# GNN layer with layer norm on one core: the order in which the first two tiles are prepared, and which engine adds epsilon for tile 0

## The reference, cut to what matters

```python
h = jnp.maximum(_layernorm(x, axis=-1), 0.0)     # x: 4096 x 256, eps 1e-5
agg = jnp.matmul(adj, h)                         # adj: 4096 x 4096
out = x + jax.nn.relu(jnp.matmul(agg, W.T) + b)  # W: 256 x 256
```

## Time and profile before

| what | value |
|---|---|
| median of 3 runs | 382.24 us (381.95 to 382.41) |
| the profiled execution's own time | 382.26 us |
| its span in the profile | 380.5 us |
| granted TensorE clock, mean | 0.998 of full speed |
| TensorE matmuls busy | 375.8 us, 99% |
| TensorE weight loads busy | 308.2 us, 81% |
| VectorE busy | 218.2 us, 57% |
| ScalarE busy | 170.9 us, 45% |
| GpSimd busy | 63.0 us, 17% |
| DMA | 80.25 MB, mean 211 GB/s |

### The profile page before, as it was taken

The page is one execution under the profiler, slowest core; times in us unless marked ns, Lnnn a source line. Parts: engine busy times, 40 slices in busy tenths (PEclk is TensorE's granted clock), DMA queues, the critical chain, the costliest instruction groups (busy, mean ns, idle before and its releaser), DMA issues.

```text
span 380.5 us, 4425 instructions
## 1 busy us (share of the span) xinstructions
PE 375.8 (99%) x1649; PEld 308.2 (81%) x1649; DVE 218.2 (57%) x293; ACT 170.9 (45%) x197; POOL 63.0 (17%) x79
## 2 busy tenths in 40 slices
PE   8999999999999999999999999999999999999996
PEld 4888888888888888888888888888888888888885
DVE  5999999994745353535564535444465344444424
ACT  4656655664543434343544343434364334343414
POOL 2787777770010000000001000000000100000000
PEclk9999999999999999999999999999999999999999
DMA  7997778669649565656565856565656675656203
GB/s 229 375 288 263 264 267 257 208 211 327 198 161 338 187 212 174 208 181 206 177 207 186 310 183 208 176 210 178 206 180 203 246 259 177 210 180 205 68 2 110
DMA packets 23062, 80.25 MB, mean 211 GB/s; under 512 B 2496, under 2 KB 3264, under 8 KB 23040
## 3 DMA queue, kind: packets, MB, share of 16 engines
q1 hardware_dynamic: 21024, 72.36, 57.9%
q0 software_dynamic: 2016, 7.60, 5.5%
HBM read 75.76 MB, written 4.19 MB: 210 GB/s over the span
## 4 chain that ended last, share of the span: by engine, by line
PE 99%; DVE 0%; ACT 0%; issue 0%
PE bank L380 92%; PE bank L421 6%; PE bank L430 1%; ACT out_sb L356 0%; DVE out_sb L293 0%; DVE warm L257 0%
## 5 line engine op out<-in xcount | busy, mean ns | idle before, releaser
L380 PE MATMUL bank<-adj_hi,h_sb 128*128 128x512 f32 x1024 | 255.2, 390 | 0.0
L224 DVE TENSOR_TENSOR adj_lo<-adj_in,adj_hi 128x1024 fp32r<-128x1024 f32 x126 | 154.2, 1224 | 138.5 <-ACT adj_hi L314 138.4
L380 PEld LDWEIGHTS bank<-adj_hi,h_sb 128*128 128x128 f32 x1024 | 192.3, 188 | 40.8 <-ACT h_sb L324 0.9
L314 ACT ACTIVATE adj_hi<-adj_in 128x1024 fp32r<-128x1024 f32 x126 | 133.5, 1059 | 159.5 <-PE bank L380 156.6
L380 PE MATMUL bank<-adj_lo,h_sb 128*128 128x512 f32 x512 | 138.0, 389 | 0.0
L380 PEld LDWEIGHTS bank<-adj_lo,h_sb 128*128 128x128 f32 x512 | 96.0, 188 | 20.6 <-DVE adj_lo L229 0.6
L204 POOL TENSOR_TENSOR rstd<-var_eps,minus_half 128x1 f32<-128x1 f32 x32 | 49.5, 1547 | 2.5
L216 POOL DMA_DIRECT2D out_t_dram<-out_sb x3 | 2.2, 723 | 209.2 <-DVE out_sb L293 209.2
L324 ACT ACTIVATE h_sb<-centred,rstd 128x256 fp32r<-128x256 f32 x32 | 16.3, 509 | 25.2 <-POOL rstd L204 25.1
L252 DVE SCALAR_TENSOR_TENSOR h_sb<-centred,rstd,h_sb 128x256 fp32r<-128x256 f32 x32 | 15.3, 479 | 0.0
L235 DVE BATCH_NORM_STATS2 stats<-x_sb 128x6 f32<-128x256 f32 x32 | 13.5, 421 | 3.2 <-DMA x_sb<-x_dram 3.2
(11 more groups left out here) (20 smaller groups left out, 31.6 us busy)
## 6 DMA issues: line engine op xcount, KB each, us to landing
adj_in<-adj_t_dram SPq DMA_DIRECT2D x126, 512.0 KB, 3.6
xt_sb<-x_t_dram POOLq DMA_DIRECT2D x4, 1024.0 KB, 7.2
x_sb<-x_dram SPq DMA_DIRECT2D x7, 512.0 KB, 6.4
out_t_dram<-out_sb POOLq DMA_DIRECT2D x3, 1024.0 KB, 5.0
adj_in<-adj_t_dram SPq DMA_DIRECT2D x4, 256.0 KB, 4.6
out_t_dram<-out_sb SPq DMA_DIRECT2D x3, 256.0 KB, 2.0
x_sb<-x_dram SPq DMA_DIRECT2D x4, 128.0 KB, 4.5
w_sb<-w_t_dram POOLq DMA_DIRECT2D x1, 256.0 KB, 5.3
```

The source lines that it names most:

```text
L224: nc.vector.tensor_tensor(adj_lo[:, k, :], adj_in[:, k, :], adj_hi[:, k, :].bitcast(fp32), ALU.subtract).then_inc(s_lo, 1)
L314: nc.scalar.activation(adj_hi[:, k, :], adj_in[:, k, :], ACT.Copy).then_inc(s_hi, 1)
L380: last = nc.tensor.matmul(bank(g, kb, c)[:], h_sb[:, t, hp, kb * P:(kb + 1) * P], adj_parts[ap][:, n % U, chunk(c)], start=(t == 0 and (hp ...
```

## The change

For the first two tiles only, the order of some instructions changes, and one instruction moves to another engine.

- VectorE adds epsilon for tile 0 with a new `tensor_scalar` on a 128x1 column, right behind tile 0's moments. GpSimd leaves out that addition for tile 0 and waits for VectorE's before it takes the power.
- VectorE makes h's low part of tile 0 before it takes tile 1's moments, centres tile 1 behind the first chunk's low part, and makes h's low part of tile 1 ahead of the low part of chunk (1,0).
- ScalarE rounds h of a tile before the adjacency: tile 0 ahead of chunk (0,0), tile 1 ahead of chunk (1,0).
- TensorE takes, in each chunk of the two tiles, the pass with h's low part second and the one with the adjacency's low part last.

```diff
             def root(t):
                 k = t % U
-                pool.wait_ge(s_mean, t + 1)
-                nc.gpsimd.tensor_tensor(var_eps[:, k:k + 1], mean_var[:, k, 1:2], eps_sb[:],
-                                        ALU.add).then_inc(s_var, 1)
+                if t > 0:
+
+                    pool.wait_ge(s_mean, t + 1)
+                    nc.gpsimd.tensor_tensor(var_eps[:, k:k + 1], mean_var[:, k, 1:2], eps_sb[:],
+                                            ALU.add).then_inc(s_var, 1)
                 pool.wait_ge(s_var, t + 1)
...
+            def first_var_eps():
+                dve.wait_ge(s_mean, 1)
+                nc.vector.tensor_scalar(var_eps[:, 0:1], mean_var[:, 0, 1:2], EPS, None, ALU.add
+                                        ).then_inc(s_var, 1)
...
-            for t in range(AHEAD):
-                moments(t)
-                centre(t)
+            moments(0)
+            first_var_eps()
+            centre(0)
+            h_rest(0)
+            moments(1)
             early_rest(0, 0)
-            h_rest(0)
+            centre(1)
             early_rest(0, 1)
+            h_rest(1)
             early_rest(1, 0)
-            h_rest(1)
             moments(2)
...
+            h_rounded(0)
             early_rounded(0, 0)
-            h_rounded(0)
             early_rounded(0, 1)
+            h_rounded(1)
             early_rounded(1, 0)
-            h_rounded(1)
             early_rounded(1, 1)
...
                     add_up(0, t, [c], 0, 0)
-                    pe.wait_ge(s_lo, made_chunk(t, c))
-                    add_up(0, t, [c], 0, 1)
                     if c == 0:
                         pe.wait_ge(s_hlo, t + 1)
-                    last = add_up(0, t, [c], 1, 0)
+                    add_up(0, t, [c], 1, 0)
+                    pe.wait_ge(s_lo, made_chunk(t, c))
+                    last = add_up(0, t, [c], 0, 1)
                 last.then_inc(s_pe, 1)
```

## The result

The changed kernel takes 383.16 us (median of 7 executions, 383.08 to 384.05) against 382.09 (7, 381.86 to 382.41). The ratio is 1.003, with a 95% interval of 1.002 to 1.0039. The forecast was 382.1, and 383.16 lies above its range. The profiled execution took 383.81 us with a span of 382.0.

A forecast was written before the change was run, and what follows sets the result against it. TensorE bounds the kernel, and its start gains only as far as VectorE's adj_rest(2) ends earlier: 12.85 instead of 13.02. Of TensorE's 0.33 us lead 0.16 is lost waiting there, 0.17 survives: 382.26 - 0.17 = 382.1 us, range 381.8 to 382.7.

The forecast's parts named there:

- step 3: ScalarE, tile 0: h rounded from about 4.40 to 4.89, before the chunk lands at 4.99, costing the chunk nothing.
- Step 4: VectorE: h_rest(0) from 4.94, moments 1 at 5.38; some 0.40 us of work moves into a 1.47 us hole.
- late case: GpSimd's first arithmetic pays 0.15 more: h rounded from 4.55, h_rest(0) from 5.09, moments 1 at 5.49; total 382.2 us.
- Steps 1 and 5 to 8: VectorE's new addition 3.50 to 3.65, then tile 1's chain; moments 2 at 9.03 instead of 9.20, adj_rest(2) ending at 12.85.
- Step 2: GpSimd, tile 0: power starts at 3.74 to 3.80, takes 0.56, `rstd` at 4.30 to 4.36 instead of 4.60; possibly 0.15 more.
- step 6: GpSimd, tile 1: addition stretched to 6.68, power 6.76 to 7.32; a late read, 0.41 of its 0.56 after it.
- the objection raised against step 2: Skill's port sharing: tile 0's power on GpSimd would wait for VectorE's centre 0 and end at 4.47.
- TensorE's own side: First real matmul at 5.86, higher clock level at about 7.1; 0.33 us ahead, reaching the matmul of 13.18 at 12.85.
- The slower rival, a power that misses its slot: Tile 1's power reads after early_rest(0,1) starts, ends at 8.24; moments 2 0.75 later than before, 383.0 us; chance 0.08.
- The blocked write: Tile 1's power can't write beside early_rest(0,1), ends near 7.87; moments 2 0.38 later than before, 382.64 us; chance 0.13.
- step 5: VectorE: aggregate 1 at 5.84, early_rest(0,0) to 6.62, centre 1 to 6.95, early_rest(0,1) 7.15 to 7.83.
- The clock: TensorE's higher level might come sooner, saving 0.20 us per matmul; the adj_rest(2) wait takes it all, no own case.

The follow-up runs named there:

- early load: Changed kernel plus a one-column ScalarE copy ahead of all others, so the table load runs early: 382.11 us, ratio 1.0001 against the kernel before.
- early load, 12 matmuls on zeros: Changed kernel with the early table load and 12 matmuls on zeros instead of 11: nine of 11 executions 382.09 to 382.28 us, others 382.53 and 382.62.
- early load, old epsilon: Changed kernel with the early table load, tile 0's epsilon addition back on GpSimd: 382.36 us, ratio 1.0001 against the kernel before.
- moments 1 first: Changed kernel with VectorE taking tile 1's moments before h's low part of tile 0, table load still late: 382.38 us, ratio 1.0004.
- only ScalarE's order: Kernel before with only the two swaps in ScalarE's list: 382.45 us, ratio 1.0007.
- all but ScalarE's order: Changed kernel with ScalarE's old order: 382.95 us, ratio 1.002 against the kernel before.
- changed, 13 matmuls on zeros: Changed kernel with 13 matmuls on zeros instead of 11: 382.97 to 383.13 us over 10 executions.
- changed, again: Changed kernel measured once more, unaltered, with 11 matmuls on zeros; also called the repeat: 383.01 to 383.15 us, median 383.11 against 382.16 before.
- the late load in the kernel before: Kernel before plus a wait for tile 0's centring ahead of the first adjacency rounding, moving the table load late: 382.27 us, ratio 1.0002.
- its 9 matmuls: Kernel before with 9 matmuls on zeros instead of 11: seven executions 381.81 to 382.29 us, five 383.06 to 383.39.
- run 7: Changed kernel with the early table load, VectorE making adjacency tile 2's low part ahead of tile 3's moments and centring: 382.52 us, ratio 1.001.

## Why the prediction was wrong, by its own steps

The step that failed is step 3: ScalarE rounds h of tile 0 from about 4.40 to 4.89, so that putting h first costs the chunk nothing. It ran from 5.45 to 5.96. The reason is the 1.28 us table load, whose row stands in the profile of before at 0.74, as ScalarE's first instruction. The prediction read ScalarE's rows from 5 us on the earlier trace rows, and took its idle time before 4.99 as free for any order. The load goes in front of whichever ACTIVATE comes first and, in all five kernels with two waits on it, behind the one that is written second, the centring.

Step 4 then turned around. It counted 0.40 us of VectorE work moved into a hole in front of 5.38, and priced a late h only by the 0.15 us of its late case. With h's low part at 5.99 instead of 4.94 it pushed moments 1 to 6.39. A delay of h by d costs d here, less the 0.04 that step 4 had to spare: 1.05 - 0.04 = 1.01. For every instruction put ahead of another in a queue there is such a price, what it costs when its input comes late; here it went no further than those 0.15 us.

The rest held. That the end of adj_rest(2) is the number to forecast is shown by all executions in which TensorE waited for it. Profiled time less that end:

| kernel | end of adj_rest(2) | time | difference |
|---|---|---|---|
| before | 13.02 | 382.26 | 369.24 |
| early load | 12.88 | 382.11 | 369.23 |
| early load, 12 matmuls on zeros | 13.00 | 382.23 | 369.23 |
| early load, old epsilon | 13.04 | 382.30 | 369.26 |
| moments 1 first | 13.19 | 382.41 | 369.22 |
| only ScalarE's order | 13.48 | 382.69 | 369.21 |
| all but ScalarE's order | 13.62 | 382.81 | 369.19 |
| changed, 13 matmuls on zeros | 13.82 | 383.04 | 369.22 |
| changed, again | 13.83 | 383.07 | 369.24 |

The nine differences lie within 0.07 us. Where TensorE did not wait for adj_rest(2) the difference is larger: 369.39 with the late load in the kernel before (12.77, 382.16) and 369.38 with its 9 matmuls (12.63, 382.01). Applied to the measured 13.87, the sum gives 383.1 us, the median of the changed kernel; the 383.81 of the first profile is 0.7 more for the clock.

- Steps 1 and 5 to 8 held with the early load, each to 0.06 us, but for early_rest(0,1): it ran from 6.85 instead of 7.15, because its chunk happened to land earlier. In run 7 it ran at 7.15, and moments 2 started at 9.07 all the same.
- Step 2 came out between its two cases. The new addition took 0.15 as taken, and the power for tile 0 took 0.59 and ended at 4.43, against 4.30 to 4.36 and 0.15 more in the late case. It ended 0.42 us behind centre 0's end (3.60 + 0.41), near the 0.41 of step 6, and so it did in the changed kernel (4.07 and 4.49). That fits a read that waits for the centring, as the objection raised against step 2 has it, but the price was only 0.03 us over the undisturbed 0.56.
- TensorE's own side was forecast too slow. With the early load the first real matmul started at 5.64 and the higher level was there at once, so TensorE could have been at the matmul of 13.18 by 10.91 + 6 x 0.2267 = 12.27, not 12.85. A wait that the prediction doesn't list, for h's high part of tile 2 until 11.74, held it, and then adj_rest(2) did until 12.93. So neither error moved the time.
- The slower rival, a power that misses its slot, did not occur: the power for tile 1 took 0.61 us in both profiles. Its size, 0.75, was near the loss, for the wrong reason.
- The blocked write fell: in the early-load run the power of tile 1 ended at 7.35, while early_rest(0,1) ran from 6.85 to 7.53 beside it. In run 7, where early_rest(0,1) ran when step 5 has it, the power ended at 7.36:

```profile
6.75 0.61 POOL L207 TENSOR_TENSOR rstd<-var_eps,minus_half 128x1 f32<-128x1 f32 x1
...
7.15 0.69 DVE L232 TENSOR_TENSOR adj_lo<-adj_in,adj_hi 128x512 fp32r<-128x512 f32 x1 [0.20 <-ACT adj_hi L332]
```

  The early-load power had started 0.11 us ahead of early_rest(0,1) and took 0.61 us, while a power recorded 0.02 us ahead of such an instruction took 1.11 us. The Trainium skill (SBUF — State Buffer, Who interferes with whom) says that the one that starts first holds the ports for its whole length, and the other is blocked. The recorded starts don't agree with that: early_rest(0,1) started second and took its usual 0.68 us beside the power, and the power of 1.11 us had started first. What decides between them is open. In run 7 a power recorded 0.02 us ahead of another two-input instruction, h's low part, was not held up either:

```profile
12.82 0.55 POOL L207 TENSOR_TENSOR rstd<-var_eps,minus_half 128x1 f32<-128x1 f32 x1
12.84 0.48 DVE L260 SCALAR_TENSOR_TENSOR h_sb<-centred,rstd,h_sb 128x256 fp32r<-128x256 f32 x1
```

- The clock was given no case of its own, because the wait for adj_rest(2) would absorb an earlier rise. That is true for an earlier rise. Of a later one TensorE's waits hide only their own length: in the repeat it could have started the matmul of 13.89 at 11.88 + 6 x 0.2267 = 13.24, so 0.65 us, and the first profile lost 0.7 beyond what its waits could hide.

The Trainium skill (ScalarE: Activation LUTs, What ACT_TABLE_LOAD costs) gives about 1283 ns for the load, and the rows here agree, 1.28 us in every profile. It also gives some 1380 ns of drain for a switch to another set of functions; at this one load of the kernel no profile shows any, since h's rounding started 0.02 us after the load's end (5.43 to 5.45).

## What to carry to other kernels

When an engine's first instruction changes, look at what is hung in front of it once per kernel: here a load of 1.28 us that lay hidden at the start and came out behind a wait. A one-column instruction with a single early wait pins it where it is free. An instruction that waits should go ahead of a ready one in the same queue only where its input is sure to be there; h's low part in front of the moments cost 1.0 us against the kernel before, nearly the whole 1.05 us by which it was late.

## What the runs showed of the hardware that was not expected

- The table load started at 0.74 us where the first ACTIVATE had one wait, and behind the centring (4.04 to 4.19 us in five kernels) where it had two. In all five the wait for the centring is written second; the two waits in the other order weren't tried.
- The same kernel's TensorE reached the higher clock level at 10.4 us in one profile and by 6.6 in another. The matmuls between are 0.43 us apart instead of 0.23, and the times differ by 0.7 us. The column of the granted clock does not show it. The stretch from 6.6 to 10.4 us (length, busy time and count of each engine, granted clock, DMA) in the first profile of the changed kernel and in the repeat:

```profile
6.60:10.40 3.80, 3.78 (x9) 3.03 (x10) 3.34 (x8) 2.25 (x5) 1.16 (x2) 1.00 0.99 368
```

```profile
6.60:10.40 3.80, 3.80 (x16) 2.83 (x17) 3.34 (x8) 2.27 (x5) 1.16 (x2) 1.00 1.02 364
```

  Both say 1.00. The count tells them apart: 9 matmuls in one and 16 in the other.
- GpSimd's power, started 0.11 us ahead of a two-input VectorE instruction of 128x512, took 0.61 us; started 0.02 ahead of one, it took 1.11; started 0.02 ahead of h's low part of 128x256, it took 0.55.
